# Second layer of a bias network on a 4 x 4 tiled TensorE: each row group's correction and second layer issued together

## The chip, the cores and the metric

The kernel runs on one core of one Trainium2 chip. The metric is the device time of one execution in microseconds; before the change its median over three runs is 914.92 us.

## The reference

Two layers of deformable attention work on x of shape (2, 128, 32, 32). Each layer makes queries by a grouped 1x1 convolution, finds 64 sampled key positions per group (8 groups) from a strided convolution, samples keys and values there, and attends from 1024 queries to 64 keys in each of 8 heads. The scores get a bias from a small network that is applied to every pair of a query and a key, and this network is most of the arithmetic:

```
pos = grid_q[:, :, None, :] - grid_kv[:, None, :, :]
bias = jnp.sign(pos) * jnp.log1p(jnp.abs(pos))
bias = jax.nn.relu(bias @ cpb_w1 + cpb_b1)
bias = jax.nn.relu(bias @ cpb_w2 + cpb_b2)
bias = (bias @ cpb_w3 + cpb_b3).reshape(b, GROUPS, H * W, Hd * Wd)
sim = jnp.einsum('bhid,bhjd->bhij', qh, kh) + bias
attn = jax.nn.softmax(sim, axis=-1)
```

The hidden width is 32. After the softmax come the output projection with a residual, and an MLP (128 to 512 to 128, gelu) with a residual.

## The kernel before, in words

The bias network runs in 256 steps g (`ALL_STEPS`): 2 layers x 2 batch entries make 4 segments, each with 4 pairs of heads (a unit), 2 halves of the 1024 queries (512 each) and 8 steps. One step handles 16 keys for 512 queries. The 128 partitions hold 4 row groups of 32 hidden units, and each row group holds 4 keys as 4 blocks of 512 columns.

The first layer is one VectorE instruction per step (`first_layer`, L576): h1 = max(hx, hy), which leaves out a term that is rank one in the hidden unit. The second layer (`layer2`, L765) adds this term back: a **correction** (L778, bf16) multiplies 32 x 32 weights `u_rows` with the key's `fy` values, broadcast over 512 columns, and the **second layer** proper (L783, float32) multiplies `w2` with `h1` on top of it in the same PSUM region. Each is 16 matmuls with 32 rows and 32 columns, one for each of the 16 tiles (row group r, column group c) of the array; row group r reads partitions 32r to 32r+31 and writes its own PSUM bank z[r]. The trace has two weight loads and two matmuls for each float32 matmul, and one of each for a bf16 matmul. So a step has 16 loads and 16 matmuls of L778 and 32 loads and 32 matmuls of L783.

ScalarE (`relu2`, L438) then takes the relu of two row groups at a time, a pair of PSUM banks, to h2, and the third layer (`layer3`, L797; 4 float32 matmuls with 128 rows and 32 columns, 8 in the trace) adds up the scores. PSUM has a ring of three pairs; `turn` waits until the pair of the ring is emptied, `filled` tells that it is written. Pair z(2g) takes row groups 0 and 1 of step g, z(2g+1) row groups 2 and 3.

TensorE's order is written out by hand: in step g come layer2(g), layer3(g-1), and then what a table of slots puts there (queries times keys L807, transposes L886, taking off the maximum L893, projections and the MLP). VectorE's first layer has three buffers and waits for the second layer of three steps before; `layer2` waits for it with `h1_ready`. The first step of all waits for `fy`, loaded by DMA.

Of the kernel before, what the change touches and what calls it, by code (L numbers as in the profile page):

```python
# [15 lines left out]
LAYERS, B, C, H, W = 2, 2, 128, 32, 32  # L16
# [18 lines left out]
ROWS = CT = 4  # L35
# [141 lines left out]
def build(nc, x_in, consts, weights, x_out, features_dram, fy_dram, reciprocals_dram):  # L177
    with ExitStack() as ctx:
        def sb(name, shape, dt=F32):
            return ctx.enter_context(nc.sbuf_tensor(name, shape, dt))  # L180
# [4 lines left out]
        def sem(name):  # L185
            return ctx.enter_context(nc.semaphore(name))
# [41 lines left out]
        u_rows = [sb(f"u_rows{l}", [128, 128], BF16) for l in range(LAYERS)]  # L228
# [35 lines left out]
        h1_ready = sem("h1_ready")  # L264
# [16 lines left out]
        def w(l, name):  # L281
            a, b = COLS[name]
            return wts[l][:, a:b]
# [5 lines left out]
        def bank(h):  # L289
            return slice(HALF * h, HALF * (h + 1))  # L290

        def pair_of(stage, n):
            return pairs[PLACE[stage, n][0]]
# [468 lines left out]
        def _(pe):  # L762
            def layer2(g):


                unit, h, t = g // UNIT_STEPS, g // STRIDES % 2, g % STRIDES
                l = unit // PAIRS // B
                if g % UNIT_STEPS == 0:
                    pe.wait_ge(fy_loaded[unit % 2], 16 * 3 * ROWS * (unit // 2 + 1))
                    pe.wait_ge(u_ready, l + 1)  # L770
                z = [pair_of("z", 2 * g + r // 2)[:, bank(r % 2)] for r in range(ROWS)]
                key = [slice(32 * r, 32 * (r + 1)) for r in range(ROWS)]
                for r in range(ROWS):
                    if r % 2 == 0:
                        turn("z", 2 * g + r // 2)
                    y = fy[unit % 2][key[r], t, H // 2 * h:H // 2 * (h + 1)]
                    for c in range(CT):
                        pe.matmul(z[r][32 * c:32 * (c + 1)], u_rows[l][key[r], 32 * c:32 * (c + 1)],  # L778
                                  y.unsqueeze(2).broadcast_to([32, H // 2, W]), start=True, stop=False)
                pe.wait_ge(h1_ready, g + 1)  # L780
                for r in range(ROWS):
                    for c in range(CT):
                        ins = pe.matmul(z[r][32 * c:32 * (c + 1)], w(l, "w2")[key[r], key[r]], h1[g % H1_BUFS][key[r], c],  # L783
                                        start=False, stop=True)
                    if r % 2:
                        filled("z", 2 * g + r // 2, ins)

            def layer3(g):

# [22 lines left out]
            def turn(stage, n):  # L812
                pair, _, before, _ = PLACE[stage, n]
                if before:
                    pe.wait_ge(pair_emptied[pair], before)

            def filled(stage, n, ins):
                ins.then_inc(pair_filled[PLACE[stage, n][0]], 1)
# [123 lines left out]
            for g in range(LAST_STEP + 1):  # L942
                if g == SEG_STEPS // 2:
                    pe.wait_ge(early_loaded[1], 16)
                    pe.wait_ge(late_loaded[1], 16)
                if g < ALL_STEPS:
                    layer2(g)
                if 1 <= g <= ALL_STEPS:
                    layer3(g - 1)
                    if (g - 1) % STRIDES == QK_STRIDE:  # L950
                        queries_keys((g - 1) // STRIDES)
                for name, n in PLAN["pe"].get(g, []):
                    stages[name](n)
# [92 lines left out]
```

## Time and profile before

| | |
|---|---|
| median of 3 runs | 914.92 us (914.75 to 918.47) |
| the profiled execution's own time | 915.2 us |
| its span | 913.2 us |
| TensorE, matmuls | 852.4 us busy, 93% |
| VectorE | 721.5 us busy, 79% |
| ScalarE | 641.6 us busy, 70% |
| mean granted TensorE clock | 0.979 |

Busy is the time in which at least one instruction of the engine is under way, and the matmuls of different tiles lie over one another: the busy time of an engine tells nothing of how many of its 16 tiles work. The rows of the timeline merge instructions of one line: start, time from the first start to the last end, engine, line, out<-in, count, and in brackets the idle time of the engine before it. A window that ends within such a group shows the group as far as it had started by then, with its count up to there.

### The profile page before, as it was taken

The numbers are of one execution on the slowest core, as the hardware profiler recorded it, in microseconds if no ns is written. First come the engines' busy times: TensorE is split into PE (matmuls) and PEld (weight loads), VectorE is DVE, ScalarE is ACT, GpSimd is POOL, SyncE is SP. The second block draws the span as 40 slices with busy tenths as digits, with TensorE's granted clock in tenths as the row PEclk, the third lists the DMA queues.
The fourth block names the chain that finished last, engine by engine and source line by source line (L and its number), as shares of the span: only waits on it lengthen the run. The fifth ranks groups of instructions, "written<-read, shape, count | busy, mean of one in ns | idle before, by whom it ended". The sixth has DMA issues, their size and how long they took to land.

```text
span 913.2 us, 34513 instructions
## 1 busy us (share of the span) xinstructions
PE 852.4 (93%) x15908; PEld 300.2 (33%) x15908; DVE 721.5 (79%) x492; ACT 641.6 (70%) x741; POOL 62.4 (7%) x40
## 2 busy tenths in 40 slices
PE   3299999899999999989999999989999999999996
PEld 1133333233333333324333333423333333333332
DVE  4789699898876689998875878989887768888831
ACT  2367678867776677986776767896777667777762
POOL 2110002310000002040000001140000000000000
PEclk8589999999999999999999999999999999999999
DMA  4301001020110102002020100102020010200001
GB/s 148 91 19 41 13 4 50 8 53 4 45 28 10 50 3 50 8 3 56 3 63 15 49 4 20 34 8 54 4 63 17 2 50 3 73 3 3 3 14 36
DMA packets 23806, 27.48 MB, mean 30 GB/s; under 512 B 15600, under 2 KB 17520, under 8 KB 23664
## 3 DMA queue, kind: packets, MB, share of 16 engines
q1 hardware_dynamic: 23664, 25.29, 10.6%
q8 instruction: 125, 2.05, 1.0%
q14 instruction: 17, 0.14, 0.1%
HBM read 23.05 MB, written 2.10 MB: 28 GB/s over the span
## 4 chain that ended last, share of the span: by engine, by line
PE 83%; DVE 7%; ACT 4%; issue 3%; SPq 1%; DMA 1%; POOL 0%; ACTq 0%; POOLq 0%
PE pair L783 29%; PE scores L797 25%; PE pair L778 10%; PE pair L930 3%; PE scores L807 3%; PE scores L893 3%; PE pair L921 3%; DVE h L576 3%; PE pair L886 2%; ACT h L438 2%; PE pair L905 2%; PE pair L831 1%; PE pair L912 1%; DVE big L680 1%; PE pair L867 1%
## 5 line engine op out<-in xcount | busy, mean ns | idle before, releaser
L438 ACT ACTIVATE h<-pair 128x1024 f32<-128x1024 f32 x512 | 496.3, 1022 | 202.1 <-PE pair L783 200.3
L576 DVE TENSOR_TENSOR h<-hx,hy 128x2048 f32<-128x2048 f32 x256 | 583.3, 2303 | 53.4 <-PE pair L783 53.3
L783 PE MATMUL pair<-h,wts 32*32 32x512 f32 x8192 | 350.9, 599 | 7.5 <-DVE h L576 7.5
L797 PE MATMUL scores<-h,wts 128*32 128x512 f32 x2048 | 274.4, 608 | 0.1
L778 PE MATMUL pair<-fy,u_rows 32*32 32x512 bf16 x4096 | 126.5, 387 | 26.7 <-DMA fy<-fy_dram 17.2
L783 PEld LDWEIGHTS pair<-h,wts 32*32 32x32 f32 x8192 | 134.5, 103 | 25.8 <-DVE h L576 10.5
L797 PEld LDWEIGHTS scores<-h,wts 128*32 128x32 f32 x2048 | 40.4, 108 | 217.0 <-issue 217.0
L778 PEld LDWEIGHTS pair<-fy,u_rows 32*32 32x32 bf16 x4096 | 40.2, 88 | 200.3 <-issue 174.2
L311 POOL TENSOR_TENSOR conv_prod<-qpad,wts 128x288 f32<-128x288 f32 x16 | 21.6, 1379 | 428.9 <-ACT qpad L465 428.9
L418 POOL TENSOR_TENSOR big<-big,hat_x 128x512 f32<-128x512 f32 x16 | 38.0, 2404 | 124.8 <-DVE big L674 124.8
L703 DVE TENSOR_REDUCE neg_max<-pair 128x8 f32<-128x512 f32 x32 | 22.1, 690 | 30.9 <-PE pair L886 30.5
L732 DVE SCALAR_TENSOR_TENSOR x<-pair,wts,x 128x512 f32<-128x512 f32 x8 | 6.0, 751 | 48.9 <-PE pair L930 48.9
L893 PEld LDWEIGHTS scores<-const,neg_max 128*64 128x64 f32 x512 | 27.3, 136 | 27.0 <-issue 23.5
L893 PE MATMUL scores<-const,neg_max 128*64 128x128 f32 x512 | 35.0, 279 | 0.8 <-DVE neg_max L703 0.8
L807 PE MATMUL scores<-qpad,keys_t 128*32 128x512 f32 x256 | 33.4, 592 | 0.0
L921 PE MATMUL pair<-work,wts 128*128 128x512 f32 x64 | 31.2, 615 | 1.4 <-DVE work L726 1.4
L531 ACT ACTIVATE big<-pair,wts 128x512 f32<-128x512 f32 x32 | 20.2, 683 | 17.4 <-PE pair L921 17.4
L930 PE MATMUL pair<-big,wts 128*128 128x512 f32 x64 | 29.5, 605 | 2.9 <-ACT big L531 2.9
L523 ACT ACTIVATE probs<-scores,wts 128x512 f32<-128x512 f32 x32 | 22.0, 688 | 10.0 <-PE scores L893 9.9
L448 ACT ACTIVATE probs<-scores,wts 128x512 f32<-128x512 f32 x32 | 22.1, 692 | 1.3 <-PE scores L797 1.3
L886 PEld LDWEIGHTS pair<-const,probs 128*128 128x128 f32 x128 | 13.4, 140 | 27.7 <-issue 26.0
L886 PE MATMUL pair<-const,probs 128*128 128x128 f32 x128 | 21.0, 287 | 0.8 <-ACT probs L448 0.8
(87 smaller groups left out, 349.3 us busy)
## 6 DMA issues: line engine op xcount, KB each, us to landing
hx<-features_dram SPq DMA_DIRECT2D x64, 128.0 KB, 2.7
hy<-features_dram SPq DMA_DIRECT2D x64, 128.0 KB, 3.1
att_den<-reciprocals_dram SPq DMA_DIRECT2D x8, 256.0 KB
wts<-weights_dram SPq DMA_DIRECT2D x2, 960.0 KB, 8.0
x<-x_dram SPq DMA_DIRECT2D x2, 512.0 KB, 5.6
fy<-fy_dram SPq DMA_DIRECT2D x64, 6.0 KB
fy<-fy_dram SPq DMA_DIRECT2D x64, 4.0 KB
fy<-fy_dram SPq DMA_DIRECT2D x64, 2.0 KB
```

Source lines behind the costliest of these rows:

```text
L418: pool.tensor_tensor(bilinear[:, k], hat_y[:, k], hat_x[:], ALU.mult).then_inc(bilinear_ready[0], 1)
L438: emptied("z", 2 * g + j, act.activation(h2[g % H2_BUFS][:, 2 * j:2 * (j + 1)].rearrange("p r n -> p (r n)"), pair_of("z", 2 * g + j)[:], ...
L448: act.activation(probs[:, unit % PAIRS, bank(h)], scores[phase % 2][:], ACT.Identity, bias=w(seg // B, "b3"))\
L576: dve.tensor_tensor(h1[g % H1_BUFS][:].rearrange("p c (y x) -> p c y x", x=W), hx[unit % 2][:, :, t].unsqueeze(2).broadcast_to([128, CT, H ...
L778: pe.matmul(z[r][32 * c:32 * (c + 1)], u_rows[l][key[r], 32 * c:32 * (c + 1)], y.unsqueeze(2).broadcast_to([32, H // 2, W]), start=True, s ...
L783: ins = pe.matmul(z[r][32 * c:32 * (c + 1)], w(l, "w2")[key[r], key[r]], h1[g % H1_BUFS][key[r], c], start=False, stop=True)
L797: ins = pe.matmul(scores[phase % 2][32 * r:32 * (r + 1)], w(l, "w3")[:, 32 * t:32 * (t + 1)], h2[g % H2_BUFS][:, r], start=t == 0, stop=t ...
L807: ins = pe.matmul(scores[phase % 2][k], keys_t[seg % 2][:, u, k], qpad[seg % 2][:, 1 + H // 2 * h:1 + H // 2 * (h + 1), 1:W + 1], start=Fa ...
L886: ins = pe.transpose(pair_of("scores_t", phase)[:, s], probs[:, unit % PAIRS, bank(h)][:, s], cst("ident"))
L893: ins = pe.matmul(scores[phase % 2][NKV * n:NKV * (n + 1), 128 * k:128 * (k + 1)], neg_max[phase % 2][:, 2 * k + n:2 * k + n + 1].broadcas ...
L921: ins = pe.matmul(pair_of("mlp_up", n)[:, bank(k)], w(half // 2 // B, "mlp_w1")[:, 128 * c:128 * (c + 1)], xn2[:, bank(half % 2)], start=T ...
L930: ins = pe.matmul(pair_of("mlp_down", half)[:, 0:HALF], w(half // 2 // B, "mlp_w2")[:, 128 * c:128 * (c + 1)], mlp_h[:, c, bank(half % 2)] ...
```

## The change

In `layer2` the two loops over row groups, first all corrections and then all second layers, become one: correction and second layer of row group 0, then of 1, 2 and 3. The wait for `h1` comes behind the correction of row group 0 (before: behind all four). The wait for the second pair of banks comes ahead of row group 2's correction, and the first pair is told filled behind row group 1's second layer. Matmuls, weights, buffers and all other engines' programs stay the same.

```diff
--- before.py
+++ after.py
@@ -770,20 +770,31 @@
                     pe.wait_ge(u_ready, l + 1)
                 z = [pair_of("z", 2 * g + r // 2)[:, bank(r % 2)] for r in range(ROWS)]
                 key = [slice(32 * r, 32 * (r + 1)) for r in range(ROWS)]
-                for r in range(ROWS):
-                    if r % 2 == 0:
-                        turn("z", 2 * g + r // 2)
+                def correct(r, **ends):
                     y = fy[unit % 2][key[r], t, H // 2 * h:H // 2 * (h + 1)]
                     for c in range(CT):
-                        pe.matmul(z[r][32 * c:32 * (c + 1)], u_rows[l][key[r], 32 * c:32 * (c + 1)],
-                                  y.unsqueeze(2).broadcast_to([32, H // 2, W]), start=True, stop=False)
-                pe.wait_ge(h1_ready, g + 1)
-                for r in range(ROWS):
+                        ins = pe.matmul(z[r][32 * c:32 * (c + 1)], u_rows[l][key[r], 32 * c:32 * (c + 1)],
+                                        y.unsqueeze(2).broadcast_to([32, H // 2, W]), **ends)
+                    return ins
+
+                def weigh(r, **ends):
                     for c in range(CT):
                         ins = pe.matmul(z[r][32 * c:32 * (c + 1)], w(l, "w2")[key[r], key[r]], h1[g % H1_BUFS][key[r], c],
-                                        start=False, stop=True)
-                    if r % 2:
-                        filled("z", 2 * g + r // 2, ins)
+                                        **ends)
+                    return ins
+
+                begins, ends = dict(start=True, stop=False), dict(start=False, stop=True)
+                turn("z", 2 * g)
+                correct(0, **begins)
+                pe.wait_ge(h1_ready, g + 1)
+                weigh(0, **ends)
+                correct(1, **begins)
+                filled("z", 2 * g, weigh(1, **ends))
+                turn("z", 2 * g + 1)
+                for r in (2, 3):
+                    correct(r, **begins)
+                    ins = weigh(r, **ends)
+                filled("z", 2 * g + 1, ins)
 
             def layer3(g):
 
```

TensorE's order in the plain step 118, between the third layer of steps 116 and 117 (before: L778 correction, L783 second layer, L797 third layer; `fy`, `u_rows` are the correction's operands, `h` the first layer's):

```order
L797 MATMUL scores<-h_1,wts 32x512 x3
L778 MATMUL pair<-fy,u_rows 32x512 [waits pair_emptied2]
L778 MATMUL pair<-fy,u_rows 32x512 x7
L778 MATMUL pair<-fy,u_rows 32x512 [waits pair_emptied0]
L778 MATMUL pair<-fy,u_rows 32x512 x7
L783 MATMUL pair<-h_0,wts 32x512 [waits h1_ready]
L783 MATMUL pair<-h_0,wts 32x512 x15
L797 MATMUL scores<-h_2,wts 32x512 [waits pair_emptied1,pair_emptied0]
```

The same step of the changed kernel (L776 correction, L782 second layer, L808 third layer):

```order
L776 MATMUL pair<-fy,u_rows 32x512 [waits pair_emptied2]
L776 MATMUL pair<-fy,u_rows 32x512 x3
L782 MATMUL pair<-h_0,wts 32x512 [waits h1_ready]
L782 MATMUL pair<-h_0,wts 32x512 x3
L776 MATMUL pair<-fy,u_rows 32x512 x4
L782 MATMUL pair<-h_0,wts 32x512 x4
L776 MATMUL pair<-fy,u_rows 32x512 [waits pair_emptied0]
L776 MATMUL pair<-fy,u_rows 32x512 x3
L782 MATMUL pair<-h_0,wts 32x512 x4
L776 MATMUL pair<-fy,u_rows 32x512 x4
L782 MATMUL pair<-h_0,wts 32x512 x4
L808 MATMUL scores<-h_2,wts 32x512 [waits pair_emptied1,pair_emptied0]
```

The last correction (row group 3) stood ahead of all sixteen second-layer matmuls and now stands behind twelve of them.

Step 18, behind the transposes of the scores (L886, in the changed kernel L897), before:

```order
L886 MATMUL pair<-const,probs 128x128 x3
L778 MATMUL pair<-fy,u_rows 32x512 [waits pair_emptied0]
L778 MATMUL pair<-fy,u_rows 32x512 x7
L778 MATMUL pair<-fy,u_rows 32x512 [waits pair_emptied1]
L778 MATMUL pair<-fy,u_rows 32x512 x7
L783 MATMUL pair<-h_0,wts 32x512 [waits h1_ready]
```

And in the changed kernel:

```order
L897 MATMUL pair<-const,probs 128x128 x3
L776 MATMUL pair<-fy,u_rows 32x512 [waits pair_emptied0]
L776 MATMUL pair<-fy,u_rows 32x512 x3
L782 MATMUL pair<-h_0,wts 32x512 [waits h1_ready]
L782 MATMUL pair<-h_0,wts 32x512 x3
L776 MATMUL pair<-fy,u_rows 32x512 x4
L782 MATMUL pair<-h_0,wts 32x512 x4
L776 MATMUL pair<-fy,u_rows 32x512 [waits pair_emptied1]
```

The wait for the second pair (here `pair_emptied1`) stood ahead of every second-layer matmul and now stands behind eight of them. The rows of VectorE, ScalarE, GpSimd and SyncE are the same in both kernels.

## Rows read from the trace of the kernel before

**Rows 1.** The page: busy times, and the chain that ended last by engine and line
```profile
PE 852.4 (93%) x15908; PEld 300.2 (33%) x15908; DVE 721.5 (79%) x492; ACT 641.6 (70%) x741; POOL 62.4 (7%) x40
...
PE 83%; DVE 7%; ACT 4%; issue 3%; SPq 1%; DMA 1%; POOL 0%; ACTq 0%; POOLq 0%
```

**Rows 2.** Timeline of all engines, a plain step, window 430:436
```profile
430.97 0.43 PE L778 MATMUL pair<-fy,u_rows 32*32 32x512 bf16 x16
...
431.20 1.34 PE L783 MATMUL pair<-h,wts 32*32 32x512 f32 x32
432.37 1.94 ACT L438 ACTIVATE h<-pair 128x1024 f32<-128x1024 f32 x2 [0.55 <-PE pair L783]
...
432.47 1.06 PE L797 MATMUL scores<-h,wts 128*32 128x512 f32 x8
432.58 2.29 DVE L576 TENSOR_TENSOR h<-hx,hy 128x2048 f32<-128x2048 f32 x1 [0.20 <-PE pair L783]
...
433.47 0.43 PE L778 MATMUL pair<-fy,u_rows 32*32 32x512 bf16 x16
```

**Rows 3.** TensorE's matmuls in this step, windows ending at 431.38, 431.60, 431.80
```profile
431.20 0.61 PE L783 MATMUL pair<-h,wts 32*32 32x512 f32 x8
...
431.20 0.91 PE L783 MATMUL pair<-h,wts 32*32 32x512 f32 x16
...
431.20 1.04 PE L783 MATMUL pair<-h,wts 32*32 32x512 f32 x24
```

**Rows 4.** TensorE's weight loads in this step, windows ending at 431.12, 431.19, 431.38
```profile
431.03 0.16 PEld L783 LDWEIGHTS pair<-h,wts 32*32 32x32 f32 x8
...
431.03 0.21 PEld L783 LDWEIGHTS pair<-h,wts 32*32 32x32 f32 x9
...
431.03 0.30 PEld L783 LDWEIGHTS pair<-h,wts 32*32 32x32 f32 x17
```

**Rows 5.** TensorE, step with late h1, windows ending at 408.06, 408.60 and 409.02
```profile
407.92 0.72 PE L783 MATMUL pair<-h,wts 32*32 32x512 f32 x16 [0.73 <-DVE h L576]
...
407.92 1.15 PE L783 MATMUL pair<-h,wts 32*32 32x512 f32 x32 [0.73 <-DVE h L576]
409.00 0.63 PE L797 MATMUL scores<-h,wts 128*32 128x512 f32 x3
```

**Rows 6.** TensorE, step behind transposes, windows ending at 99.00, 99.24, 99.42, 99.49, 100.5
```profile
98.71 0.41 PE L778 MATMUL pair<-fy,u_rows 32*32 32x512 bf16 x8
...
98.71 0.71 PE L778 MATMUL pair<-fy,u_rows 32*32 32x512 bf16 x16
99.05 0.66 PE L783 MATMUL pair<-h,wts 32*32 32x512 f32 x8
...
99.05 0.79 PE L783 MATMUL pair<-h,wts 32*32 32x512 f32 x12
...
99.05 1.04 PE L783 MATMUL pair<-h,wts 32*32 32x512 f32 x16
...
99.05 1.47 PE L783 MATMUL pair<-h,wts 32*32 32x512 f32 x32
100.45 0.64 PE L797 MATMUL scores<-h,wts 128*32 128x512 f32 x4
```

**Rows 7.** Lines L783 and L778 over the span: ns of one matmul, min/median/max
```profile
L783 PE MATMUL pair<-h,wts x8192: 584/587/1057, 43.5 to 878.6; 32*32 32x512 f32 x200
...
L778 PE MATMUL pair<-fy,u_rows x4096: 384/385/626, 43.1 to 877.7; 32*32 32x512 bf16 x196
```

**Rows 8.** Who waited for whom: us in total, times, longest
```profile
DVE h L576 <- PE pair L783: 53.3, 80, 2.1
...
PEld pair L778 <- ACT h L438: 12.7, 39, 1.1
...
PEld pair L783 <- DVE h L576: 10.5, 10, 1.9
...
PEld pair L778 <- ACT work L496: 8.4, 3, 2.8
```

## The prediction

> **What bounds the kernel now.** I read the page first: TensorE is busy 93% of the span and holds 83% of the chain that ended last; VectorE holds 7% and ScalarE 4% [rows 1]. So the length of TensorE's step sets the time. A plain step takes 2.50 us, correction to correction (430.97 to 433.47), in three parts [rows 2]: correction to second layer 0.23 us (431.20), second layer to third layer 1.27 us (432.47), third layer to the next correction 1.00 us. ScalarE takes 1.94 us of it and VectorE 2.29, and both idle before their work, waiting for TensorE. The sum below is about one stretch: from the correction's start to the third layer's start, 1.50 us now.
>
> **How TensorE runs these matmuls.** A busy share does not say how many of the 16 tiles work, so I cut the step with windows. In the plain step 8 second-layer matmuls start at 431.20, no further one by 431.38, 16 have started by 431.60, 24 by 431.80, 32 at the end [rows 3]. Where h1 came late, 16 start within 0.14 us, and all 32 by 408.60 [rows 5]. A float32 matmul is two passes on its tile. One pass takes about 0.43 us from the start of the first to that of the second, since the two sets of 16 in [rows 5] lie 0.43 apart (the first set is 0.72 long with all its starts, 1.15 with the second). A tile cannot run both passes at once, so the first 16 starts are the first passes of 16 tiles. This gives two readings:
>
> 1. A matmul whose tile is busy does not hold up later ones on other tiles: the second pass of the first tile stands second in the order and starts behind sixteen first passes.
> 2. It reaches ahead only so far. In the plain step row groups 0 and 1 start at 431.20, but groups 2 and 3 only after 431.38, though their corrections had started 0.03 us behind the others'. A correction's record lasts 0.385 us [rows 7], so the first one ends at 430.97 + 0.385 = 431.36. In front of group 2 stand 32 instructions of the correction (16 loads, 16 matmuls) and 32 of groups 0 and 1: 64. The weight loads fit: 8 by 431.12, one more by 431.19; the next 8, by 431.38, are those of the second passes of groups 0 and 1 [rows 4]. So I read: 64 instructions at most are under way, and one enters for each that ends **at the head**. Had finished instructions anywhere made room, the correction's 16 loads, each over in 0.1 us, would have let in four more tiles by 431.19; one load came in.
>
> The step behind the transposes says the same. There corrections 2 and 3 come 0.31 us late: none had started by 99.00, and the last started at 98.71 + 0.71 - 0.385 = 99.04, so all of them at some 99.02 to 99.04. Second-layer matmuls: eight by 99.24, twelve by 99.42, sixteen by 99.49 [rows 6]. Groups 0 and 1 of the correction had ended at 98.71 + 0.41 = 99.12 and made room for 16 instructions, just row group 2. Row group 3 had to wait until the late corrections ended, 99.02 + 0.385 = 99.40.
>
> **The change in a plain step.** The order is now, in instructions: correction 0 (8), second layer 0 (16), correction 1 (8), second layer 1 (16), correction 2 (8), second layer 2 (16), correction 3 (8), second layer 3 (16). The first 64 reach to the middle of row group 2. When correction 0 ends, at +0.39, 8 leave and the rest of group 2 enters. Then the head is a float32 matmul of row group 0, which started at +0.23:
>
> - its first pass ends, by the record of 0.587 us [rows 7], at 0.82, and lets in a single correction of group 3;
> - its second pass starts at 0.23 + 0.43 = 0.66 and ends at 0.66 + 0.59 = 1.25. Only now do the other three corrections of group 3 enter, at about 1.28 with the 0.03 us seen above between an end and an entry;
> - correction to second layer 0.23: 1.51; second pass 0.43 later: 1.94, with the spread of three tiles 1.97;
> - from the last start of the second layer to the third layer 0.52 us: the last one ends at 431.20 + 1.34 = 432.54, started 0.587 earlier at 431.95, and the third layer starts at 432.47 [rows 2]. This gives 2.49 us.
>
> So the stretch grows from 1.50 to 2.49 us, **+0.99 us** per step. The work is the same; row group 3 runs nearly by itself behind the others. 256 steps: +253.4 us. Bounds of the term: 0.90, if a place comes free not at the record's end but 0.52 after the start, as the third layer does (0.07 earlier, rounded down); 1.05, if the last tiles of group 3 enter 0.03 us apart, as ends and entries lie.
>
> **What it gives back.** A longer step hides waits [rows 8]: TensorE for relu of the step before 12.7 us (39 times, the 0.31 us of [rows 6]): the second pair is now asked for before row group 2, which is not what the end of the step hangs on: gone. For late h1 10.5 us (10 times): VectorE's 2.29 us stand against a step of 3.49 instead of 2.50, and its three buffers fill: gone. For L496 8.4 us (3 times): shrinks by about a step's growth each, some 4 us stay. Together 27 us, bounds 15 (half stays) and 32 (all). That corrections 1 to 3 stand behind the wait for h1 costs nothing once h1 is early; if VectorE still ran late it would add to those ten steps the 0.23 us now hidden, 2 us. VectorE's 53.3 us of waiting and ScalarE's idle time grow and cost nothing. The earlier `filled` of the first pair lets ScalarE start its relu about 1 us ahead of the second, which nobody needs.
>
> **Sum**: 915.2 + 253.4 - 27 = 1141.6, taken as **1141 us**. The profiled execution is 0.3 us above the median, which is nothing here. This case by its own bounds: 915.2 + 256 x 0.90 - 32 = 1114 to 915.2 + 256 x 1.05 - 15 = 1169.
>
> **The rivals.**
>
> *Room is made anywhere* (0.14). If the limit is on 32 matmuls (16 + 16 in the plain step) and each one that ends makes room, the loads of [rows 4] are explained as well. Then corrections 0 to 2 end at 0.39 and correction 3 starts at 0.41, its second layer at 0.64, last pass 1.07 to 1.10, third layer 1.62: +0.12 per step, +31 us, and about half of the waits stay: 915.2 + 31 - 13 = 933 us; 919 if all go. Against it: in all rows what ends first also stood first, so they don't decide. The Trainium skill, page "TensorE: Matmul & The Clock Gate", section "The mechanism", has a window of 64 instructions for reordering and matmuls that end strictly in program order; by that the case above stands and this one falls, and the count of 64 agrees with [rows 3, 4].
>
> *First passes keep the order* (0.08). If only the second pass may lag and correction 1 must wait until second layer 0 has started, each row group begins 0.23 later than the one before: second layer 3 at 0.92, second pass 1.35, third layer 1.90, +0.40: 915.2 + 102 - 30 = 987 us. No row shows a correction passing a waiting second layer.
>
> *Strict order* (0.05). If correction 1 cannot start before second layer 0's last pass, each row group adds 0.66: 4 x 0.66 + 0.52 = 3.16, +1.66: 915.2 + 425 - 30 = 1310 us. The same section of the Trainium skill says that matmuls also start in program order, without reordering. By that rule the time would be these 1310 us; the trace disagrees, as sixteen tiles start before the first one's second pass [rows 5].
>
> *Faster* (0.04). If row groups 2 and 3 now start late, not for want of places, but because all corrections are in front of them, the change takes that away: every row group runs 0.23 + 0.43 + 0.52 = 1.18 us instead of 1.50, and the relu starts early. 256 x 0.32 = 82 us, 833 us, unless VectorE bounds it. This decides if row group 3's correction starts within 0.1 us of the step's. Against it stands [rows 6], where row group 2 got in the moment places came free.
>
> The clock is a risk within these: granted 0.979 on the mean of the span, and a step in which one row group works alone could be given the lower level of 1.2 GHz; no row here has such a step. 0.03, above the range.
>
> **How the numbers follow.** The first case has 0.66. A measurement of this kernel can tell 0.5%, 4.6 us. Faster holds its rival, 0.04; within 0.5% a part of the second case if it gives back nearly all, 0.04; slower the rest, 0.92. The likeliest case alone would be 1114 to 1169. To hold 8 in 10 the range must reach down over 987 to 933; above, it ends at 1169, and 1310 is left out: 928 to 1169.
>
> **What would show it.** Plain step about 3.5 us. Twelve corrections start within 0.1 us, one more near +0.85, the last three near +1.28; 24 second-layer matmuls start before +0.9, the last near +1.97; third layer at +2.49. TensorE's waits for relu and h1 near zero, VectorE's for TensorE well over 53 us. It is wrong if correction 3 starts near +0.41 (933) or correction 1 only behind second layer 0's first or second passes (987, 1310).

## The result and the profile after

The changed kernel takes 1144.47 us (median of 4 runs, 1143.79 to 1150.15) against 914.84 us before: ratio 1.2507, 95% interval [1.2472, 1.2542]. Predicted were 1141 us. Four of the medians below (the pairs, the run without row group 2, one single matmul moved forward, the wide correction) count one far slower execution each, which the ratios leave out, so the ratio is the one to go by.

The page of the changed kernel, busy times and chain (before: [rows 1]):

```profile
PE 1092.5 (96%) x15908; PEld 389.7 (34%) x15908; DVE 722.6 (63%) x492; ACT 676.0 (59%) x741; POOL 54.2 (5%) x40
...
PE 94%; DVE 1%; ACT 1%; DMA 1%; SPq 1%; issue 1%; POOL 0%; ACTq 0%; POOLq 0%
```

The counts are the same as before, 15908 matmuls and 15908 loads; TensorE is busy 240 us longer with them and holds 94% of the chain instead of 83%. A reader who looks at the busy share alone would call 96% a better used engine than 93%.

A plain step of the changed kernel (step 118; L776 correction, L782 second layer, L808 third layer), all of TensorE's matmuls, window 536.6:539.2 (before: [rows 2]):

```profile
536.62 0.48 PE L776 MATMUL pair<-fy,u_rows 32*32 32x512 bf16 x12
536.85 1.20 PE L782 MATMUL pair<-h,wts 32*32 32x512 f32 x23
537.46 0.37 PE L776 MATMUL pair<-fy,u_rows 32*32 32x512 bf16 x1
537.50 0.59 PE L782 MATMUL pair<-h,wts 32*32 32x512 f32 x1
537.89 0.40 PE L776 MATMUL pair<-fy,u_rows 32*32 32x512 bf16 x3
537.91 1.23 PE L782 MATMUL pair<-h,wts 32*32 32x512 f32 x8
539.08 0.64 PE L808 MATMUL scores<-h,wts 128*32 128x512 f32 x4
```

Twelve corrections start at once, one at +0.84 us, three at +1.27; 24 matmuls of the second layer have started by +0.88, then nothing more of it until the eight of row group 3 (and its last tiles only after their corrections); the third layer comes at +2.46. The last of the eight starts at 537.91 + 1.23 - 0.587 = 538.55, which is +1.94. The last second pass of row group 2 starts at 537.50 and its record ends 0.59 us later, at +1.47, so from there on row group 3 has the array to itself. 250 of 255 such stretches that the trace lets me measure are 2.45 to 2.46 us long (before, 195 of 255 are 1.50 us, the others longer, mostly by the waits of [rows 8]).

Waits, who for whom, us in total, times, longest (before: [rows 8]):

```profile
DVE h L576 <- PE pair L782: 189.1, 129, 3.1
...
PEld pair L776 <- ACT work L496: 6.3, 3, 2.1
...
PEld pair L782 <- DVE h L576: 1.4, 1, 1.4
```

TensorE waits for h1 1.4 us instead of 10.5, and of the 12.7 us that the correction waited for relu L438 no row is left among the sixty longest. The list does charge 61.2 us of idle weight loads ahead of the third layer to L438, but these delay nothing: in 252 of 255 steps, before and after alike, the third layer starts 0.52 us behind the last start of the second layer. VectorE waits for it 189 us instead of 53.

### The profile page after: what moved, and what is told of

It is laid out like the page before. It is cut to its first block, busy times and chain, and to the rows that moved or that the text cites. A ratio compares the mean times of both kernels' runs of the same rounds, so it can differ in the third digit from the quotient of the medians.

```text
span 1142.5 us, 34513 instructions
## 1 busy us (share of the span) xinstructions
PE 1092.5 (96%) x15908; PEld 389.7 (34%) x15908; DVE 722.6 (63%) x492; ACT 676.0 (59%) x741; POOL 54.2 (5%) x40
## 4 chain that ended last, share of the span: by engine, by line
PE 94%; DVE 1%; ACT 1%; DMA 1%; SPq 1%; issue 1%; POOL 0%; ACTq 0%; POOLq 0%
PE pair L782 42%; PE scores L808 22%; PE pair L776 14%; PE scores L904 3%; PE pair L941 3%; PE pair L932 2%; PE scores L818 2%; PE pair L897 2%; PE pair L916 1%; PE pair L842 1%; PE pair L923 1%; PE pair L878 1%; SPq L371 1%; PE pair L866 1%; DMA const<-consts_dram 0%
## 5 line engine op out<-in xcount | busy, mean ns | idle before, releaser
L438 ACT ACTIVATE h<-pair 128x1024 f32<-128x1024 f32 x512 | 523.9, 1024 | 366.0 <-PE pair L782 336.1
L576 DVE TENSOR_TENSOR h<-hx,hy 128x2048 f32<-128x2048 f32 x256 | 590.7, 2321 | 189.2 <-PE pair L782 189.1
L782 PE MATMUL pair<-h,wts 32*32 32x512 f32 x8192 | 595.5, 596 | 1.1 <-DVE h L576 1.1
L776 PE MATMUL pair<-fy,u_rows 32*32 32x512 bf16 x4096 | 322.1, 387 | 21.1 <-DMA fy<-fy_dram 17.5
L808 PE MATMUL scores<-h,wts 128*32 128x512 f32 x2048 | 276.1, 612 | 0.0
L776 PEld LDWEIGHTS pair<-fy,u_rows 32*32 32x32 bf16 x4096 | 115.2, 88 | 349.1 <-issue 341.3
L782 PEld LDWEIGHTS pair<-h,wts 32*32 32x32 f32 x8192 | 212.0, 104 | 14.0 <-DVE h L576 1.4
L808 PEld LDWEIGHTS scores<-h,wts 128*32 128x32 f32 x2048 | 40.5, 108 | 216.8 <-issue 155.7
L418 POOL TENSOR_TENSOR big<-big,hat_x 128x512 f32<-128x512 f32 x16 | 29.9, 1897 | 149.5 <-DVE big L674 149.5
L897 PEld LDWEIGHTS pair<-const,probs 128*128 128x128 f32 x128 | 13.4, 140 | 27.7 <-issue 26.0
L897 PE MATMUL pair<-const,probs 128*128 128x128 f32 x128 | 21.0, 287 | 0.8 <-ACT probs L448 0.8
```

Of the source, the lines that this page charges most:

```text
L418: pool.tensor_tensor(bilinear[:, k], hat_y[:, k], hat_x[:], ALU.mult).then_inc(bilinear_ready[0], 1)
L438: emptied("z", 2 * g + j, act.activation(h2[g % H2_BUFS][:, 2 * j:2 * (j + 1)].rearrange("p r n -> p (r n)"), pair_of("z", 2 * g + j)[:], ...
L576: dve.tensor_tensor(h1[g % H1_BUFS][:].rearrange("p c (y x) -> p c y x", x=W), hx[unit % 2][:, :, t].unsqueeze(2).broadcast_to([128, CT, H ...
L776: ins = pe.matmul(z[r][32 * c:32 * (c + 1)], u_rows[l][key[r], 32 * c:32 * (c + 1)], y.unsqueeze(2).broadcast_to([32, H // 2, W]), **ends)
L808: ins = pe.matmul(scores[phase % 2][32 * r:32 * (r + 1)], w(l, "w3")[:, 32 * t:32 * (t + 1)], h2[g % H2_BUFS][:, r], start=t == 0, stop=t ...
L897: ins = pe.transpose(pair_of("scores_t", phase)[:, s], probs[:, unit % PAIRS, bank(h)][:, s], cst("ident"))
```

## The experiments

The theory on trial, called the **head theory** in the expectations: TensorE has at most 64 instructions under way (loads and matmuls); tiles work independently within these; a place comes free only when the instruction at the head, the oldest, has ended. Rivals are the place of the last correction, the amount of work ahead of it, and the wait for h1. Each edit is to the order in `layer2` (`weigh` is the second layer of a row group). For every run I give the stretch from the first correction to the third layer in a plain step, read from its trace, beside the time.

**1. One second-layer group moved forward.** The order of the kernel before, but:

```diff
 correct(0)
 pe.wait_ge(h1_ready, g + 1)
+weigh(0)
 correct(1)
 correct(2)
 correct(3)
-weigh(0)
 weigh(1)
```

> The order of the kernel before with one group moved: second layer 0 stands directly behind correction 0, the corrections 1, 2 and 3 follow, then second layers 1, 2 and 3. Head theory: only the 8 instructions of correction 0 leave at 0.39 us, then a float32 group is the head until 1.25, second layer 3 starts at 1.27 or later, third layer at 2.30, about 1097 us, as bad as the order in pairs. Rival theory, the place of the last correction: it stands behind one group of the second layer only, so a third of the growth stays, about 991 us.

Measured 1099.58 us, ratio 1.198 [1.192, 1.205]. The timeline of a plain step, TensorE, windows 511.44:512.6 and 511.44:513.9:

```profile
511.46 0.46 PE L776 MATMUL pair<-fy,u_rows 32*32 32x512 bf16 x16
511.68 1.24 PE L782 MATMUL pair<-h,wts 32*32 32x512 f32 x21
...
511.68 2.16 PE L782 MATMUL pair<-h,wts 32*32 32x512 f32 x32
513.77 0.64 PE L808 MATMUL scores<-h,wts 128*32 128x512 f32 x4
```

All 16 corrections start within 0.46 - 0.385 = 0.08 us, so none is late. Still only 21 second-layer matmuls have started by 512.6; the other 11 come after +1.27, and the third layer at +2.31. The place of the last correction falls as a cause: nothing is late but the free places.

**2. One single matmul moved forward.** As in 1, but only the second layer of row group 0, key block 0 stands behind correction 0; the other three blocks stay where they were.

```diff
 correct(0)
 pe.wait_ge(h1_ready, g + 1)
+weigh(0, cs=(0,))
 correct(1)
 correct(2)
 correct(3)
-weigh(0)
+weigh(0, cs=(1, 2, 3))
```

> The order of the kernel before with a single matmul moved forward: second layer of row group 0, key block 0 (4 of the step's 96 instructions) directly behind correction 0; then corrections 1 to 3 and the rest as before. Head theory: that one float32 matmul is at the head from 0.39 to 1.25 us, so the last tile of second layer 2 and all of second layer 3 start at 1.27 or later, third layer at 2.31, about 1098 us, as much as with the whole group moved. Rival (the loss grows with the number of second-layer matmuls that stand ahead of corrections): a quarter of the 184 us of the run with the whole group moved, about 961 us.

Measured 1098.7 us, ratio 1.196 [1.193, 1.198]; windows 511.54:512.6 and 511.54:514:

```profile
511.55 0.44 PE L776 MATMUL pair<-fy,u_rows 32*32 32x512 bf16 x16
511.78 1.24 PE L782 MATMUL pair<-h,wts 32*32 32x512 f32 x21
...
511.78 2.16 PE L782 MATMUL pair<-h,wts 32*32 32x512 f32 x32
513.87 0.64 PE L809 MATMUL scores<-h,wts 128*32 128x512 f32 x4
```

The same picture to 0.01 us, from 4 instructions of 96. One float32 matmul at the head holds the places of 24 finished correction instructions behind it for its two passes.

**3. One correction moved back.** The opposite: of the 16 corrections, the last (row group 3, key block 3) goes behind second layer 0.

```diff
-correct(3)
+correct(3, cs=(0, 1, 2))
 pe.wait_ge(h1_ready, g + 1)
 weigh(0)
+correct(3, cs=(3,))
 weigh(1)
```

> The order of the kernel before with a single matmul moved back: the correction of row group 3, key block 3 (2 instructions) behind second layer 0. Head theory: 30 correction instructions stand at the head, leave at 0.39 to 0.43 us and let in second layer 2 and all but the last two instructions of second layer 3; those come at 0.84, before their tile is free at about 0.98. Third layer at 1.50 to 1.52, 915 to 921 us. Rival (a correction behind a float32 group waits for it): 1.27 + 0.23 + 0.43 + 0.52 = 2.45 us, over 1090 us.

Measured 915.23 us, ratio 0.999 [0.997, 1.001]; window 431.38:433:

```profile
431.39 0.46 PE L776 MATMUL pair<-fy,u_rows 32*32 32x512 bf16 x16
431.62 1.34 PE L782 MATMUL pair<-h,wts 32*32 32x512 f32 x32
432.89 0.64 PE L809 MATMUL scores<-h,wts 128*32 128x512 f32 x4
```

1.50 us as before. The correction starts with the others (all within 0.46 - 0.385 = 0.08 us): it passes the waiting second layer of row group 0. So mixing bf16 corrections and float32 matmuls in the order costs nothing by itself here.

**4. As much work left out, once at the head and once not.** The changed kernel without the second layer's matmuls of row group 0, and without those of row group 2 (the correction of that group then closes its PSUM region).

```diff
-weigh(0, **ends)
```

```diff
-weigh(2, **ends)
```

> The changed kernel, with the second layer's matmuls of row group 0 left out (its region of PSUM holds the correction alone). Head theory: two corrections stand at the head, leave at 0.39 us and let in all of second layer 3; third layer at 1.42 us, about 897 us. Rival theory (the amount of work behind which the last group stands): the same time as the run that leaves out row group 2's.

> The changed kernel, with the second layer's matmuls of row group 2 left out: as much work as in the run that leaves out row group 0's. Head theory: the head is second layer 0, half of second layer 3 enters only at 1.27 us, third layer at 2.22 us, about 1084 us. Rival theory: the same time as the run without row group 0's second layer.

Measured 900.6 us without row group 0's (ratio 0.983 [0.978, 0.988]) and 1093.14 us without row group 2's (1.190 [1.180, 1.200]). The last two rows of the plain step, without row group 0's, window 429.61:431.2:

```profile
429.86 1.26 PE L782 MATMUL pair<-h,wts 32*32 32x512 f32 x24
431.05 0.64 PE L807 MATMUL scores<-h,wts 128*32 128x512 f32 x4
```

and without row group 2's, window 515.67:518:

```profile
515.91 2.09 PE L782 MATMUL pair<-h,wts 32*32 32x512 f32 x24
517.93 0.64 PE L807 MATMUL scores<-h,wts 128*32 128x512 f32 x4
```

The same 24 matmuls take 1.26 or 2.09 us. The stretch is 1.43 us and 2.25 us. With the same amount of work, some 190 us (the difference of the two ratios) depend on which group stands at the head.

**5. Orders in between.** In pairs: corrections 0 and 1, second layers 0 and 1, corrections 2 and 3, second layers 2 and 3. One ahead: corrections 0, 1, second layer 0, correction 2, second layer 1, correction 3, second layers 2 and 3.

```diff
 correct(0)
 correct(1)
 weigh(0)
+correct(2)
 weigh(1)
-correct(2)
 correct(3)
 weigh(2)
 weigh(3)
```

(- in pairs, + one ahead)

> Order in pairs: corrections 0 and 1, second layers 0 and 1, corrections 2 and 3, second layers 2 and 3. Head theory (64 instructions under way, places come free only at the head): all corrections start at once, the two corrections at the head end at 0.39 us and let in second layer 2, but second layer 3 waits for the second passes of second layer 0 and starts at 1.27. Third layer at 2.25 us behind the first correction (before 1.50, changed kernel 2.46), about 1091 us. Rival theory, the place of the last correction: it stands behind two groups of the second layer instead of three, so two thirds of the growth stay, about 1068 us, and second layer 3 starts with its correction.

> Order with the corrections one ahead: corrections 0, 1, second layer 0, correction 2, second layer 1, correction 3, second layers 2 and 3. The first 64 instructions are now all corrections and second layers 0 and 1, as in the kernel before, only in another order. Head theory: the two corrections at the head leave at 0.39 us and let in second layer 2; second layer 3 starts at 1.27, third layer at 2.25, about 1091 us. Rival (what counts is which 64 instructions come first, not their order among themselves): third layer at 1.50 as before, about 915 us.

In pairs 1095.95 us, ratio 1.194 [1.187, 1.201]; one ahead 1094.25 us, 1.195 [1.191, 1.198]. The trace of the pairs is that of a second run of the same kernel, of which was expected:

> The order in pairs again, for its trace: corrections 0 and 1, second layers 0 and 1, corrections 2 and 3, second layers 2 and 3. Head theory: all sixteen corrections start within 0.15 us, second layer 2 at 0.41, second layer 3 (but for one first pass at 0.84) at 1.27, third layer at 2.25 to 2.28.

Its one execution took 1090.36 us. Both orders have the third layer at +2.28. The pairs' timeline, windows 508.62:509.8 and 508.62:511:

```profile
508.63 0.53 PE L776 MATMUL pair<-fy,u_rows 32*32 32x512 bf16 x16
508.86 1.27 PE L782 MATMUL pair<-h,wts 32*32 32x512 f32 x25
...
508.86 2.12 PE L782 MATMUL pair<-h,wts 32*32 32x512 f32 x32
510.91 0.64 PE L808 MATMUL scores<-h,wts 128*32 128x512 f32 x4
```

One ahead, windows 513.99:515.2 and 513.99:516.3:

```profile
514.22 1.27 PE L782 MATMUL pair<-h,wts 32*32 32x512 f32 x25
...
514.22 2.12 PE L782 MATMUL pair<-h,wts 32*32 32x512 f32 x32
516.28 0.64 PE L808 MATMUL scores<-h,wts 128*32 128x512 f32 x4
```

The order one ahead is the sharper test: its first 64 instructions are the same as in the kernel before, only sorted otherwise, and still it costs 179 us. What is first to leave decides.

**6. 64 instructions or 32 matmuls?** Every load goes with one matmul here, so the traces before could not tell. The kernel before, with a second, useless weight load for each correction:

```diff
                     for c in range(CT):
+                        pe.ldweights(u_rows[l][key[r], 32 * c:32 * (c + 1)], tile_position=(32 * r, 32 * c))
                         pe.matmul(z[r][32 * c:32 * (c + 1)], u_rows[l][key[r], 32 * c:32 * (c + 1)],
```

> What fills the places: 64 instructions, or 32 matmuls? The kernel before, with each of the 16 corrections' weight loads issued twice (the first is of no use): the correction is 48 instructions, but still 16 matmuls. If instructions count: only second layer 0 fits at once, 4 matmuls by 0.38 us instead of 8; the others enter from 0.41 on, third layer at 1.56 to 1.58 instead of 1.50, some 15 to 20 us more, about 932 us. If matmuls count: 8 second-layer matmuls by 0.38 us, third layer at 1.50 to 1.52, 915 to 920 us.

Measured 935.24 us, ratio 1.020 [1.016, 1.025]; windows 439.47:439.85 and 439.47:441.1:

```profile
439.71 0.61 PE L784 MATMUL pair<-h,wts 32*32 32x512 f32 x5
...
439.71 1.40 PE L784 MATMUL pair<-h,wts 32*32 32x512 f32 x32
441.04 0.64 PE L798 MATMUL scores<-h,wts 128*32 128x512 f32 x4
```

Five second-layer matmuls start with the corrections instead of the eight of [rows 3]: four of row group 0, and one more in the places of the first loads at the head, which end early. The third layer comes at 441.04 - 439.48 = 1.56 us. Instructions count, loads among them.

**7. The wait for h1 alone.** The order of the kernel before, with the wait moved to where the change has it.

```diff
 correct(0)
+pe.wait_ge(h1_ready, g + 1)
 correct(1)
 correct(2)
 correct(3)
-pe.wait_ge(h1_ready, g + 1)
 weigh(0)
```

> The order of the kernel before, with only the wait for h1 moved behind correction 0, as the change moves it. Head theory: no part in the growth; only in the steps where h1 comes late are three corrections no longer done by then, 10 steps of about 0.23 us: 915 to 918 us. Rival (the wait behind the first correction holds TensorE up): over 925 us.

Measured 917.54 us, ratio 1.0034 [1.0018, 1.0051]: 3 of the 230 us, by the interval 2 to 5. The plain stretch is 1.50 us.

**8. Fewer instructions in front.** All four key blocks of a row group share `fy`, so its correction can be one matmul with 128 columns of weights.

```diff
-                    for c in range(CT):
-                        pe.matmul(z[r][32 * c:32 * (c + 1)], u_rows[l][key[r], 32 * c:32 * (c + 1)],
-                                  y.unsqueeze(2).broadcast_to([32, H // 2, W]), start=True, stop=False)
+                    pe.matmul(z[r], u_rows[l][key[r]], y.unsqueeze(2).broadcast_to([32, H // 2, W]), start=True, stop=False)
```

> The order of the kernel before, with the correction of a row group as one matmul of 32 rows and 128 columns (weights u_rows of all four keys at once, the same fy values stream to all) instead of four of 32 x 32: 8 instructions instead of 32. Head theory: second layers 2 and 3 no longer wait for places, except for half of group 3. If matmuls of 128 and of 32 columns may lie over one another, third layer at about 1.40 us, 890 us; if the array must be empty between them, corrections end at 0.39 and the second layer takes the 1.08 us of the step with late h1: 1.48, about 911 us. If the other shape costs more than that: over 915 us.

Measured 927.32 us, ratio 1.0125 [1.0104, 1.0146]: a miss. Windows: 444.68:446.2 in a step without waits, its first relu (window 444.68:447.5), and a step with a wait, 436:440:

```profile
444.69 0.40 PE L775 MATMUL pair<-fy,u_rows 32*128 32x512 bf16 x4
445.02 1.14 PE L780 MATMUL pair<-h,wts 32*32 32x512 f32 x32
446.09 0.65 PE L804 MATMUL scores<-h,wts 128*32 128x512 f32 x4
...
446.21 1.94 ACT L438 ACTIVATE h<-pair 128x1024 f32<-128x1024 f32 x2 [1.33 <-PE pair L780]
```

```profile
436.06 0.57 PE L775 MATMUL pair<-fy,u_rows 32*128 32x512 bf16 x4
...
436.56 1.14 PE L780 MATMUL pair<-h,wts 32*32 32x512 f32 x32
437.63 0.17 PEld L804 LDWEIGHTS scores<-h,wts 128*32 128x32 f32 x8 [0.84 <-issue]
...
437.76 1.94 ACT L438 ACTIVATE h<-pair 128x1024 f32<-128x1024 f32 x2 [0.65 <-PE pair L780]
```

The stretch does shrink to 1.40 us here, in 98 of 255 steps, and all 32 matmuls of the second layer follow one another without the gap of [rows 3] (1.14 us instead of 1.34). But they start 0.33 us behind the correction instead of 0.23, so that 1.40 was also a forecast is chance. In this step ScalarE's first relu begins 446.21 - 444.69 = 1.52 us after the correction (before 432.37 - 430.97 = 1.40, [rows 2]); of the 0.12 us the later start of the second layer accounts for 0.10. The relu takes 1.02 us and ends at +2.54, while the step has shrunk from 2.50 to 2.41 us, so the next step's corrections 2 and 3, which need that pair, come 0.57 - 0.385 = 0.18 us late (second window; its own relu then begins at +1.70). The kernel before had 433.47 - 432.37 - 1.02 = 0.08 us to spare there. 91 stretches are 1.57 to 1.58 us long. Across the span the loads of L775 waited 26.9 us for L438 (12.7 before) and its matmuls 6.1 us (3.6 before).

**9. A version on this basis.** In the 112 steps without other work near, corrections 0 and 1 of the next step are issued behind this step's second layer, in the same tiling and ahead of the third layer; 16 instructions instead of 32 then stand in front.

```diff
+                if not starts_early(g):
+                    correct_pair(g, 0)
+                correct_pair(g, 1)
                 pe.wait_ge(h1_ready, g + 1)
...
+                if starts_early(g + 1):
+                    correct_pair(g + 1, 0)
```

> A version built on the head theory, from the order of the kernel before: in the 112 steps with no other work near, corrections 0 and 1 of the next step are issued behind this step's second layer and ahead of the third layer, so that only 16 instructions stand ahead of the second layer, not 32. Head theory: second layers 0 and 1 start at 0.03 to 0.08, 2 at 0.23, 3 at 0.41 us; the second layer's last pass starts at about 0.90, and the next step's corrections 0 and 1 enter at 1.07 when second layer 0 leaves the head and stream until 1.37: third layer at 1.43 to 1.46 us instead of 1.50, a gain of 0.04 to 0.07 us in 112 steps, 907 to 911 us. Rival (what is taken from the front is added at the end in full, 0.21 us, or the pair's relu comes too late): 915 us or more.

Measured 914.24 us, ratio 0.9975 [0.9960, 0.9990]: clear of one, but only 0.25%, and short of the 907 to 911 us that were expected. Of the kernels with the full computation it is the only one that is faster than the kernel before by an interval clear of one. Of relu L438 its waits say:

```profile
PEld pair L777 <- ACT h L438: 100.6, 166, 1.5
...
PE pair L777 <- ACT h L438: 3.7, 7, 0.6
```

The loads of the correction wait 100.6 us for relu instead of 12.7 [rows 8], but beside running matmuls: the matmuls themselves wait 3.7 us for it, as before (3.6). So this is not the place of the rest. The trace shows where: in a run of such steps one takes 0.04 us less than before from third layer to third layer (61 of 77), and the last one of a run 0.07 less (28 of 35). But the step before each run issues its own sixteen corrections and eight for the next step, and takes 0.13 to 0.14 us more (32 of 34), some 4 us in all. In part the work taken from the front is added at the end, as the rival had it.

## Why the prediction was right

1141 us were predicted, 1144.47 measured, and by the mechanism named. Step by step:

- **What bounds.** TensorE's step sets the time [rows 1, 2]. The 229.3 us by which the span grew (913.2 to 1142.5) lie in the stretch from the correction's start to the third layer's: added up over the steps in both traces it grew by 228 us. The stretches from the third layer to the next correction are 1 us shorter together, and what lies ahead of the first correction and behind the last third layer is 2 us longer.
- **The reading of [rows 3 to 6]**, 64 instructions, room only at the head, tiles independent: shown by runs 1 to 6. The rival "room is made anywhere" (933 us) would have had correction 3 at +0.41; it is at +0.84 and +1.27. "First passes keep the order" (987) and "strict order" (1310) would have had correction 1 behind second layer 0; twelve corrections start within 0.10 us. "Faster" falls with them. The Trainium skill, page "TensorE: Matmul & The Clock Gate", section "The mechanism", gives a window of 64 and matmuls that end in program order. The 64 agrees with these runs. Of the order of the ends, what agrees is that places come free in program order; the records themselves do not end so: in run 3 all corrections are over by 431.39 + 0.46 = 431.85, and the second layer of row group 0 ahead of the last one, which starts at 431.62, is not over before 431.62 + 0.587 = 432.21. Its other statement there, that matmuls also start in program order, does not: in run 3 the sixteenth correction starts 0.15 us ahead of the second layer that stands before it in the program. The 1310 us that the prediction gave for that statement hold the row groups back but not the tiles of one group; had every second pass held up the next tile too, sixteen tiles would have taken some 16 x 0.43 = 6.9 us a step, by estimate; the kernel before, with 1.50 us from correction to third layer, refutes that already.
- **The term per step**: 0.99 us predicted, 0.96 measured (2.46 against 1.50). The entry at +1.25 was right (seen: 1.27, with 1.28 forecast for the entry); the spread of the last tiles was counted 0.03 us too much. 256 x 0.03 = 8 us too much in the sum.
- **What it gives back**: 27 us predicted. Of the 31.6 us of [rows 8] some 8 are left (6.3 for L496, 1.4 for h1), so 24 came back. Against them stands something the sum put at nothing: the start. Between 53 and 67 us the granted clock is at the level of 1.2 GHz in the changed kernel's trace, and at 2.4 GHz in that of the kernel before. The windows 53:67 of the kernel before, then of the changed kernel (us, busy of PE, PEld, DVE, ACT, POOL, clock, DMA share, GB/s):

```profile
53.00:67.00 14.00, 14.00 (x316) 5.53 (x300) 10.86 (x7) 10.13 (x15) 0.00 (x0) 1.00 0.02 4
```

```profile
53.00:67.00 14.00, 14.00 (x140) 4.15 (x140) 3.77 (x2) 4.10 (x4) 0.00 (x0) 0.50 0.01 2
```

  Two stretches of 4.59 us lie in it. The fifth step's correction starts at 68.31 us in the changed kernel and at 58.70 in the kernel before, 9.6 us later. Four steps' growth explains 3.8 of it; the other 6 us are the start. So 246 (256 x 0.96) less 24 plus 6 make 228, and 1 more lies behind the last third layer: 229. That the order of the change brings the longer low level is not shown. In both kernels TensorE had matmuls under way in all of the 14 us. In the traces of runs 1, 2 and 5, whose orders are nearly as slow, the granted clock is 1.00 in the whole of 50:67.
  Against the sum the term per step is 8 us less, and what came back, the start and the end are 3, 6 and 1 us more. These nearly cancel: that 1141 lies only 3 us from the result is luck.
- **The wait for h1** behind the first correction was costed at nothing to 2 us; run 7 measured 0.34% (3 us, 2 to 5 by the interval) for it in the order of the kernel before, a little more.

The clock risk (0.03) hardly came: 0.976 on the mean against 0.979, mostly at the start. The plain steps kept the higher level, though row group 3 works alone at the end of each, but for 3.4 us at 746 us; the kernel before has a stretch as long, at 166 us.

What stays open: whether the limit is one queue or a sum of several that happens to be 64. In runs 1 to 6 one queue forecasts the third layer to 0.03 us; nothing here could look inside it.

## What to carry to other kernels

When small matmuls run side by side on tiles of the array, order them so that what ends first stands first: short ones (here bf16) in a block ahead of the long ones (here float32). An instruction that is done gives nothing back while a longer one is ahead of it, and a single float32 matmul (two passes, 0.43 + 0.587 = 1.02 us) in front of 24 short instructions cost as much as four of them (some 180 us here). Count the loads and both passes of a float32 matmul against 64; and before shortening such a step, look how much time the releases that it needs had to spare (0.08 us in run 8).

## What the runs showed that was not expected

- The size of the cliff: 4 of 96 instructions moved, +20% (run 2); 2 of 96 moved the other way, 0% (run 3).
- Matmuls of 32 x 128 tiles are followed by 32 x 32 ones only after 0.33 us, against 0.23 between two of 32 x 32 with the same 512 columns (run 8). The 0.10 us go with the change of tiling; no run separates it from the width of the correction itself. I had two cases for it, 0.23 and 0.39, and neither was it.
- In one trace of the changed kernel TensorE spends 14 us at the lower clock while at least one matmul is always under way, and the kernel before is just as busy by this measure at the higher one. The busy share of the profile did not tell the two levels apart.
